# The up products of a feed-forward block: read by VectorE from their PSUM bank, instead of copied out by ScalarE first

## The reference

```python
x = x + tanh(g_xattn) * layernorm(attention(layernorm(x), ctx, mask) @ Wo.T + bo) * gamma + beta   # in outline
x = x + tanh(g_ffn) * ffn(layernorm(x))

def ffn(x):                                  # _activation_quant: rows scaled to 127 and rounded
    h = silu(bitlinear(x, w1)) * bitlinear(x, w2)    # 256 -> 704, twice
    return bitlinear(h, w3)                          # 704 -> 256
```

## Time and profile before

| | |
|---|---|
| median of 3 runs | 1347.72 us (1346.01 to 1348.87) |
| profiled execution, first to last instruction (span) | 1347.5 us, 0.2 us from the median |
| TensorE busy | 1303.3 us, 97% |
| VectorE busy | 1114.3 us, 83% |
| ScalarE busy | 964.8 us, 72% |
| GpSimd busy | 443.3 us, 33% |
| mean granted TensorE clock | 0.985 |

### The profile page before, as it was taken

One profiled execution on the slowest core, in us unless ns is written; L12 is line 12 of the kernel. 1 busy time (PEld: TensorE's weight loads), 2 busy tenths in 40 slices (PEclk: granted clock), 3 DMA queues, 4 the chain that ended last, 5 costly groups with the idle time before them and its releaser, 6 DMA issues.

```text
span 1347.5 us, 48025 instructions
## 1 busy us (share of the span) xinstructions
PE 1303.3 (97%) x19984; PEld 1207.4 (90%) x19984; DVE 1114.3 (83%) x2248; ACT 964.8 (72%) x1617; POOL 443.3 (33%) x751
## 2 busy tenths in 40 slices
PE   5999999999999999999999999999999999999993
PEld 4988999999999999999999999999999999999982
DVE  5878888888888888888888888888888888888864
ACT  3776777677777777777777777767777777777761
POOL 3323333323334322333332334332333332333310
PEclk9999999999999999999999999999999999999985
DMA  8867677667777767777767767766767776767630
GB/s 227 195 154 169 162 187 169 161 166 171 164 185 174 166 164 168 173 169 178 168 164 174 173 157 187 173 162 164 174 154 191 172 166 165 173 165 177 148 74 9
DMA packets 142511, 222.15 MB, mean 165 GB/s; under 512 B 29194, under 2 KB 135630, under 8 KB 142286
## 3 DMA queue, kind: packets, MB, share of 16 engines
q1 hardware_dynamic: 128632, 198.78, 61.3%
q0 software_dynamic: 12288, 19.69, 6.7%
q10 hardware_dynamic: 1366, 0.53, 0.2%
HBM read 54.00 MB, written 3.28 MB: 43 GB/s over the span
## 4 chain that ended last, share of the span: by engine, by line
PE 89%; SPq 4%; DVE 3%; DMA 2%; issue 1%; ACT 1%; POOL 0%; DVEq 0%; POOLq 0%
PE sc L1239 22%; PE pvb L1259 20%; PE cb L1294 19%; PE cb L1280 18%; SPq L309 4%; PE mb L1351 3%; PE mb L1320 2%; PE mb L1329 2%; DMA k_st<-k_lo 2%; PE mb L1366 2%; PE mb L1358 1%; DMA c_in<-in_ctxT 0%; PE mb L1313 0%; DVE c_hi L754 0%; PE mb L1335 0%
## 5 line engine op out<-in xcount | busy, mean ns | idle before, releaser
L556 ACT ACTIVATE e_sb<-sc 121x800 f32<-121x800 f32 (+1 forms) x768 | 645.6, 847 | 147.9 <-PE sc L1239 135.3
L1239 PE MATMUL sc<-q_st,k_st 96*121 96x200 f32 (+1 forms) x3072 | 472.2, 276 | 7.1 <-issue 3.0
L1239 PEld LDWEIGHTS sc<-q_st,k_st 96*121 96x121 f32 (+1 forms) x3072 | 411.6, 185 | 34.6 <-issue 8.5
L793 DVE TENSOR_SCALAR e_sb<-e_sb,hi_b 121x1600 f32<-121x1600 f32 (+1 forms) x384 | 399.6, 1048 | 0.8 <-ACT e_sb L556 0.8
L1259 PE MATMUL pvb<-e_sb,v_sb 121*32 121x100 f32 x12288 | 287.6, 251 | 0.0
L1259 PEld LDWEIGHTS pvb<-e_sb,v_sb 121*32 121x32 f32 x12288 | 266.3, 110 | 22.2 <-issue 19.0
L1294 PE MATMUL cb<-wv_hi,c_hi 128*121 128x256 f32 (+1 forms) x768 | 222.1, 289 | 1.6 <-DVE k_lo L784 1.3
L784 DVE SCALAR_TENSOR_TENSOR k_lo<-cb,bk_c,k_hi 128x484 fp32r<-128x484 f32 (+1 forms) x192 | 134.5, 700 | 107.5 <-ACT k_hi L568 107.5
L1294 PE MATMUL cb<-wv_hi,c_lo 128*121 128x256 f32 (+1 forms) x768 | 216.1, 281 | 0.0
L1294 PE MATMUL cb<-wv_lo,c_hi 128*121 128x256 f32 (+1 forms) x768 | 216.0, 281 | 0.0
L470 POOL DMA_DIRECT2D q_st<-bd_hi x256 | 164.0, 644 | 123.7 <-DVE bd_lo L839 120.7
(11 more groups left out here) (160 smaller groups left out, 1508.5 us busy)
## 6 DMA issues: line engine op xcount, KB each, us to landing
k_st<-k_hi SPq DMA_DIRECT2D x512, 121.0 KB, 2.9
c_in<-in_ctxT SPq DMA_DIRECT2D x64, 484.0 KB, 4.0
k_st<-k_lo SPq DMA_DIRECT2D x256, 121.0 KB, 2.9
k_st<-k_hi SPq DMA_DIRECT2D x256, 119.0 KB, 3.5
c_in<-in_ctxT SPq DMA_DIRECT2D x32, 476.0 KB, 4.7
k_st<-k_lo SPq DMA_DIRECT2D x128, 119.0 KB, 3.2
q_st<-bd_hi POOLq DMA_DIRECT2D x256, 50.0 KB, 3.3
q_st<-bd_lo POOLq DMA_DIRECT2D x128, 50.0 KB, 3.3
```

Source lines behind the costliest of these rows:

```text
L556: nc.scalar.activation(e_sb[e_slot(b, n)][0:TL[n], k * SW:(k + 1) * SW].rearrange("p (o c) -> p o c", o=2), sc[q % NSC][0:TL[n], :, 0:2 * PW],
L793: V.tensor_scalar(e, e, E_LO, hi_b[b.par][0:TL[n], n:n + 1], ALU.max, ALU.min).then_inc(clip_done, 1)
L1239: last = T_.matmul(sc[q % NSC][0:TL[n], e // 2, (e % 2) * PW:(e % 2 + 1) * PW], k_st[st_slot(b, n // TPC)][:, pr // NQ, pr % NQ, t0:t0 + T ...
```

## The change

ScalarE no longer copies the up halves (`ffn_up` and the tile `us` are gone). VectorE's `hidden_up` takes the product from the PSUM bank, multiplies by the scale (`tiny[:, 5:6]`, one value for each row, made by GpSimd) and by `th` in one operation. It waits for TensorE's product and for GpSimd's scale, where it waited for ScalarE's copy; and TensorE's g1 waits for VectorE's `hb0` (the first half's `hidden_up`) where it waited for ScalarE's `u0`.

```diff
-            def ffn_up(b, i, mb=mb):
-                cols = slice(i * FH, (i + 1) * FH)
-                act.wait_ge(pe_post, D_T.after(b, f"u{i}"))
-                nc.scalar.activation(us[:, cols], mb[0:S, 0:FH], ACT.Copy, scale=tiny[:, 5:6]).then_inc(act_post, 1)
...
-                    if prev and n in (9, 10):
-                        ffn_up(d, n - 9)
...
-            def hidden_up(b, i):
+            def hidden_up(b, i, bank=mb):
                 cols = slice(i * FH, (i + 1) * FH)
-                dve.wait_ge(act_post, D_A.after(b, f"u{i}"))
+                dve.wait_ge(pe_post, D_T.after(b, f"u{i}"))
+                dve.wait_ge(pool_post, D_P.after(b, "cu"))
                 d_wait(b, f"ha{i}")
-                dv(V.tensor_tensor(gs[:, cols], th[:, cols], us[:, cols], ALU.mult))
+                dv(V.scalar_tensor_tensor(gs[:, cols], bank[0:S, 0:FH], tiny[:, 5:6], th[:, cols], ALU.mult, ALU.mult))
...
                 else:
-                    pe.wait_ge(act_post, D_A.after(b, "u0"))
+                    pe.wait_ge(dve_post, D_V.after(b, "hb0"))
```

More of the change, by code:

```diff
@@ L173, in flamingo_block @@
         x2T = sb("x2T", [P, KT, S], bf16)
-        th_p, gs_p, us_p = sb("th", [P, F]), sb("gs", [P, F]), sb("us", [P, F])
-        th, gs, us = th_p[0:S, :], gs_p[0:S, :], us_p[0:S, :]
+        th_p, gs_p, w2_p = sb("th", [P, F]), sb("gs", [P, F]), sb("w2_p", [P, F])
+        th, gs = th_p[0:S, :], gs_p[0:S, :]
         hq = sb("hq", [S, FT * P], bf16)
@@ L185, in flamingo_block @@
         w1s = [th_p[:, :], gs_p[:, :]]
-        w2s = [us_p[:, :], w3q[:, :, :].rearrange("p k n -> p (k n)").bitcast(f32)[:, 0:F]]
+        w2s = [w2_p[:, :], w3q[:, :, :].rearrange("p k n -> p (k n)").bitcast(f32)[:, 0:F]]
         w3s = care[:, 0:FT * H]
@@ L235, in flamingo_block @@
         D_T = Steps("delta", "x2T", "g0", "u0", "g1", "u1", "hT", "y")
-        D_A = Steps("x2T", "t0", "g0", "u0", "t1", "g1", "u1", "hT")
+        D_A = Steps("x2T", "t0", "g0", "t1", "g1", "hT")
         pieces = [slice(a, min(a + H, CW)) for a in range(0, CW, H)]
@@ L680, in passes @@
                     ffn_gate(e, i, sc[0][:, i, :])
-                    ffn_up(e, i, sc[1][:, i, :])
                 h_turned(e)
@@ L1196, in passes @@
                     hidden_gate(e, i)
-                    hidden_up(e, i)
+                    hidden_up(e, i, sc[1][:, i, :])
                 for step in (h_max, h_scale, h_round, h_quant, result):
```

## The result

The changed kernel takes 1384.96 us in the median of four runs (1384.23 to 1386.08), the kernel before, measured beside it, 1346.87 us in the median of four; the ratio is 1.0291, with a 95% interval of 1.0273 to 1.0310. It is slower by 38 us.

The account below looks back on a forecast made before the run. TensorE was taken to bound every batch. Waits at g1 of 38.1 + 2.24 + 0.70 us, less 4.0 given back, make 37.0 us: 1384.5 us on the span, 1384.7 us median, range 1377 to 1395.

Parts of the forecast that it names:

- The bound: Every batch: TensorE, busy 40.00 us of 40, sets the time; any wait in mid-batch adds its full length.
- The removed copies: ScalarE: dropping 62 copies of 0.586 us and two more, some 37 us, gains nothing, since TensorE never waits for them.
- The new operation: VectorE's multiplication reading PSUM with a per-row scale takes 0.575 us, 0.05 us more than the 0.53 of now.
- The wait at g1: TensorE stands still for VectorE's hb0: 1.36 us in 28 batches, 2.24 in the first, 0.70 in the last but one.
- The sum: Whole run: 28 x 1.36 plus 2.24 plus 0.70, less 4.0, makes 37.0 us on the 1347.5 us span.
- The end of the run: Last batch with attention beside it: no wait; very last batch without attention: zero, give or take 0.3 us.
- What is given back: Small delays across 28 batches, mostly waits for the last stacked keys, overlap the standing still: all 4.0 us, possibly none.
- The base: Starting time: the kernel before's profiled span of 1347.5 us, with the median taken as 0.2 us above the span.
- The faster one: VectorE reaches hidden_up 1.36 us earlier relative to g1, so no wait; 1343.7 us at best; chance 0.03.
- The slower operation: VectorE's PSUM read takes up to 1.05 us, waits grow by 0.48 us each, 14 us in all: 1399 us; chance 0.06.
- The clock: TensorE's clock falls to half level after each wait, adding 2.9 us in 30 batches: 1472 us; chance 0.03.
- signs of being wrong: L934 begins earlier than 0.7 us after TensorE's arrival, batch under 41.2 us despite the wait, or TensorE's clock dips.

Follow-up runs that it names:

- the kernel with the wait alone: Kernel before with only g1's condition changed: it waits for VectorE's hb0, not ScalarE's u0; copies and SBUF multiplication stay. 1383.56 us, ratio 1.0289.
- the kernel with the order alone: Kernel before, with only VectorE's first multiplication moved ahead of the context split; g1 still waits for ScalarE. 1345.99 us, ratio 1.0016.
- the copies kept: Changed kernel with ScalarE still copying the up halves, values unread, though VectorE waits for them. 1383.57 us, ratio 1.0290.
- the smaller wait: Changed kernel with VectorE's first multiplication moved ahead of the two statistics operations of n = 9. 1362.72 us, ratio 1.0128.

## Why the prediction was right

**The bound.** TensorE, 40.00 busy of 40 in the kernel before, is busy 40.05 of 41.40 now. Right: its standing still goes into the time one for one.

**The removed copies, worth nothing.** Right, and shown by the kernel that keeps them.

**The new operation.** 0.575 us was forecast from L967 and L784, 0.581 is measured. The bound from below, L935, lacked both the PSUM read and the per-row scale. A row of the kernel before tells the two apart: an operation of 256 columns that reads PSUM and has a fixed number in place of the per-row scale takes 0.417 us, where L967 with the scale takes 0.475.

```profile
L879 DVE SCALAR_TENSOR_TENSOR dl<-mb,bo_t 100x256 f32<-100x256 f32 x32 | 13.4, 417 | 2.1 <-PE mb L1329 2.1
```

So by these rows the 0.05 us over L935 go with the scale and not with PSUM. The Trainium skill (VectorE: DVE Perf Modes, section on the TRN2 errata) has a larger fixed part for reading PSUM, by which the prediction got an estimate of 0.60 us. The 0.581 measured lies nearer to the rows' value, but 0.02 us are too little to decide by it alone.

**The wait at g1.** The forecast was that g1 comes 1.36 us later (0.73 of lateness, the operation, and 0.05 of release). The wait on record is 1.34 us in 28 batches; the first is 2.22 against 2.24, the last but one 0.64 against 0.70, and the last has none, as forecast. But a batch grew by 1.40 us, 0.06 more than the recorded wait: in the kernel before, g1 started while the last value matmul was still in the record, which no longer happens. The forecast counted from the start of g1, so 1.40 is what its 1.36 has to be compared with.

**The sum.** 37.0 us forecast on the profiled span, 36.7 measured (1384.2 - 1347.5). Its parts: up to the second g1 3.8 us (149.90 - 146.08), where 2.24 + 1.36 = 3.6 had been counted; from there to g1 of the last but one 1159.45 - 1123.74 = 35.7, where 27 x 1.36 + 0.70 - 4.0 = 33.4 had been counted; after it 74.85 us against 77.68, 2.8 less, where nothing had been counted. The middle came out 2.3 us above the forecast and the end 2.8 us below it, so the closeness of the sum is in part luck.

**The end of the run** did not get shorter by the change. The stretches from the last but one g1 to the last, and from there on, in the kernel before, in the changed kernel and in the one with the multiplication ahead of `clip`, where TensorE does not stand still (the clock is the third number from the end):

```profile
1269.82:1307.84 38.02, 35.66 (x574) 32.69 (x570) 27.15 (x53) 25.41 (x40) 8.18 (x11) 0.91 0.49 112
1307.84:1347.50 39.66, 17.31 (x196) 12.70 (x192) 20.34 (x48) 9.38 (x17) 2.71 (x7) 0.61 0.03 8
```

```profile
1309.35:1345.88 36.53, 34.35 (x569) 31.28 (x569) 26.04 (x51) 24.78 (x38) 7.47 (x10) 0.95 0.48 106
1345.88:1384.20 38.32, 15.94 (x196) 11.03 (x192) 20.20 (x48) 8.28 (x14) 2.86 (x7) 0.65 0.03 9
```

```profile
1268.26:1303.16 34.90, 33.09 (x573) 29.99 (x569) 27.46 (x52) 24.75 (x38) 8.11 (x10) 1.00 0.52 118
```

The stretch takes 38.02 us at a granted clock of 0.91, 36.53 at 0.95 and 34.90 at 1.00. It is no matter of the wait: the kernel with the wait alone has 0.91 there, and the kernel with the order alone, which has no wait, 1.00. The scatter from one execution of the same kernel to the next goes the same way: of the 21 later runs of the kernel before the longest, 1347.65 us, has a mean granted clock of 0.985, and the shortest, 1341.45 us, 0.990.

**What is given back** was the weakest term. Forecast: all 4.0 us of small delays, mostly waits for the stacked keys. The 28 batches of the changed kernel hold 1159.45 us less 27 x 41.39 and one of 40.70, which leaves 1.2 us of small delays where the kernel before had 4.0: 2.8 us are given back. The other profiled executions agree: 0.8 to 1.3 us are left in those with a standing still, 2.2 to 4.0 us in those without. What the delays consist of was misread. Of the 4.0 us in the kernel before, TensorE waits 0.7 us for the keys, and 1.2 us ahead of the shared bank's matmuls, put down to issue:

```profile
PE mb L1351 <- issue: 1.2, 2, 0.7
PE sc L1239 <- DMA k_st<-k_lo: 0.7, 3, 0.3
```

In these batches of the changed kernel both are gone. Over the whole trace the waits for the keys are not smaller, as had been expected, but 3.2 us against 2.0, since one at the start, at 43.2 us, takes 2.48.

The medians have to be read in the same way. With the 0.06 us that a wait costs beyond its record, 1.8 us over 30 waits, the waits come to 40.2 us in the kernel with the wait alone (28 x 1.25 + 2.28 + 1.10 = 38.4 recorded), 42.1 with the copies kept (40.3) and 21.9 with the smaller wait (20.1). The three stand over the kernel before by 38.8, 39.3 and 18.0 us. So 1.4, 2.8 and 3.9 us are given back, with some 2 us of doubt in each.

**The base** was high. The profiled execution that the prediction worked from had a span of 1347.5 us, where the 23 and 21 later runs of the kernel before have spans of 1343.0 and 1342.5 us in the median and take 1.8 us more than their spans, not 0.2. Their medians are 1344.75 and 1344.28 us. On 1344.75 the forecast loss of 37.0 us would have given 1381.8 us, 3.2 below the measured 1384.96, and the sum with nothing given back, 41.0, 1385.8 us. The mechanism was right and the size near, but that 1384.7 lies 0.3 us from the measurement is luck: a base that was 3 us high made up for waits that were counted a little too small and a give-back that was counted a little too large.

**The rivals.** The faster one had VectorE come earlier through the upper key part: it came at the same distance, 1.74 us of idling before and after. The slower operation did not come: 62 of them average 0.581 us. The clock stayed at 1.00 through a batch with the wait. Of the signs of being wrong, the nearest was the first: the new operation begins 0.70 us after TensorE's arrival (729.09 - 728.39), just at the bound.

## What to carry to other kernels

Who releases a shared buffer is part of a change's cost, even if the work itself gets cheaper: look up in the trace when the new releaser will be through, with all that its list holds ahead, and compare that with the moment at which the bound engine comes. Here a reader that was 1.9 us early was replaced by one that was 1.3 us late, 30 times. Such a wait is mended either by moving the releasing piece ahead of work that nobody waits for, or by giving the waiting engine other work first; and if the engine relieved was never waited for, the mended version is only as fast as what it started from.

## What was not expected

Operations of VectorE are now and then lengthened by about half a microsecond while GpSimd is at work. In the kernel with the multiplication ahead of `clip`, the remainder of the context split, 1.14 us elsewhere, took 1.67 us in 20 batches. VectorE and GpSimd there:

```profile
705.94 1.67 DVE L752 TENSOR_TENSOR c_lo<-c_in,c_hi 128x952 fp32r<-128x952 f32 x1
...
706.11 0.53 POOL L470 DMA_DIRECT2D q_st<-bd_lo  x1
706.64 0.53 POOL L470 DMA_DIRECT2D q_st<-bd_hi  x1
707.19 1.01 POOL L434 TENSOR_TENSOR x_res<-x_in,beta_t 100x256 f32<-100x256 f32 x1
```

The excess of 0.53 us is the length of one of GpSimd's transfer issues, but an issue beside the operation is not enough to lengthen it. In 28 batches of the kernel before, two issues lie at the same distance behind the start of the split, and it took 1.14 or 1.15 us:

```profile
706.74 1.14 DVE L760 TENSOR_TENSOR c_lo<-c_in,c_hi 128x952 fp32r<-128x952 f32 x1
...
706.92 1.06 POOL L470 DMA_DIRECT2D q_st<-bd_hi  x2
```

In all 20 long ones GpSimd's own operation on x (L434) follows the two issues at once. L941, two inputs in SBUF, had once taken 1.05 us instead of 0.53, with only issues beside it, and did so again at the same place in the kernel with the wait alone (1.04 us); one clipping of the kernel with the multiplication ahead of `clip`, with a single tensor input, took 1.58 us instead of 1.05. The new operation, with one input in PSUM, took 0.57 to 0.59 us in every batch of the changed kernel. The Trainium skill (SBUF — State Buffer, section on the two separate sides) has VectorE and GpSimd lock each other out of a shared pair of ports, each for a whole instruction, when VectorE reads two inputs from SBUF and GpSimd's instruction reads SBUF too. No run here shows whether an issue reads SBUF, and these rows do not settle whether that rule is at work: the cause stays open. The long splits cost no time that the runs can tell: the kernel that has them stands at a ratio of 1.0000 to the kernel before.
